# Attention plus mixture of experts on one core: GpSimd's part of the routed slots, unrolled, with its index copies taken out and a weight copy moved in

## What is computed

```python
x = x + gamma * softmax_attention(layernorm(x), ctx, ctx)      # 4 x 512 tokens, 512 wide, 8 heads
t = layernorm(x).reshape(2048, 512)
shared = (silu(t @ sw_gate) * (t @ sw_up)) @ sw_down            # 1408 hidden
top_w, top_i = top_k(softmax(t @ router_w.T), 2)                # 8 experts, 2 for each token
routed[e] = (silu(t @ w_gate[e]) * (t @ w_up[e])) @ w_down[e]   # 352 hidden
out = x + sum_e combine[:, e] * routed[e] + sigmoid(t @ shared_gate_w) * shared
```

## Time and profile before

| | us |
|---|---|
| median of 3 runs | 990.9 (988.89 to 993.4) |
| span of the profiled execution | 980.4 |
| the 39 slots, from the end of the shared expert (about 647) on | about 333 |

### The profile page before, as it was taken

One profiled execution on the slowest core, in us unless ns is written; L12 is line 12 of the kernel. 1 busy time (PEld: TensorE's weight loads), 2 busy tenths in 40 slices (PEclk: granted clock), 3 DMA queues, 4 the chain that ended last, 5 costly groups with the idle time before them and its releaser, 6 DMA issues.

```text
span 980.4 us, 14857 instructions
## 1 busy us (share of the span) xinstructions
PE 887.9 (91%) x4560; PEld 743.1 (76%) x4560; DVE 608.1 (62%) x920; ACT 537.9 (55%) x918; POOL 487.4 (50%) x500
## 2 busy tenths in 40 slices
PE   5798999989989999999999999999888888888993
PEld 3587777778777888888888888888777777777882
DVE  5678787878845633421222121258999998999881
ACT  5588878787855321121121111258777777777781
POOL 5687788777610000273100000027777778887774
PEclk9899999999999999999999999999999999999996
DMA  9334434443633323000400055556333333333333
GB/s 138 80 127 132 134 125 137 120 148 109 226 120 117 97 76 128 1 1 25 118 11 1 0 175 177 177 176 209 66 65 64 64 64 64 64 64 64 65 55 43
DMA packets 70143, 93.78 MB, mean 96 GB/s; under 512 B 16137, under 2 KB 35593, under 8 KB 70098
## 3 DMA queue, kind: packets, MB, share of 16 engines
q1 hardware_dynamic: 60338, 72.73, 24.9%
q0 software_dynamic: 9760, 20.49, 12.1%
HBM read 65.59 MB, written 27.60 MB: 95 GB/s over the span
## 4 chain that ended last, share of the span: by engine, by line
PE 43%; POOL 15%; issue 13%; ACT 2%; POOLq 2%; DMA 2%; DVE 1%; SPq 0%; ACTq 0%; DVEq 0%
PE bank L1348 8%; PE bank L1349 8%; PE bank L1350 8%; POOL sidx L615 5%; POOL wd L631 4%; PE bank L1362 4%; PE bank L1364 4%; PE bank L1363 4%; POOL gidx L607 2%; POOL out L624 2%; POOL xg L610 1%; DMA out<-y,sidx 1%; PE bank L1242 1%; ACT pb L681 1%; PE bank L1415 1%
## 5 line engine op out<-in xcount | busy, mean ns | idle before, releaser
L1036 DVE TENSOR_TENSOR sg<-bank,sg 128x512 f32<-128x512 f32 x44 | 30.4, 692 | 208.7 <-PE bank L1350 200.0
L1348 PE MATMUL bank<-x_hl,wsp 128*128 128x512 f32 x352 | 137.1, 390 | 0.0
L1350 PE MATMUL bank<-x_hl,wsp 128*128 128x512 f32 x352 | 137.0, 389 | 0.0
L1349 PE MATMUL bank<-x_hl,wsp 128*128 128x512 f32 x352 | 136.9, 389 | 0.0
L610 POOL DMA_INDIRECT xg<-x_normed_rows,gidx x39 | 40.9, 1048 | 186.9 <-PE bank L1372 158.8
L1152 DVE TENSOR_TENSOR wg<-wex,wg 128x1408 fp32r<-128x1408 f32 x39 | 112.0, 2871 | 12.4 <-ACT wg L813 12.4
L624 POOL DMA_INDIRECT out<-y,sidx x39 | 96.0, 2462 | 38.4 <-POOL sidx L615 18.4
L787 ACT ACTIVATE sg<-bank 128x512 f32<-128x512 f32 x44 | 26.3, 598 | 158.4 <-PE bank L1350 158.4
L687 ACT ACTIVATE pth<-bank 128x512 fp32r<-128x512 f32 x128 | 73.3, 598 | 49.2 <-PE bank L1242 47.7
L593 POOL DMA_INDIRECT slot_rows<-msrc,posi x32 | 32.8, 1025 | 134.2 <-DVE posi L1143 124.7
L934 DVE TENSOR_TENSOR ptl<-bank,pth 128x512 fp32r<-128x512 f32 x128 | 85.9, 682 | 18.7 <-ACT pth L687 18.4
(11 more groups left out here) (160 smaller groups left out, 2420.0 us busy)
## 6 DMA issues: line engine op xcount, KB each, us to landing
cd<-in_ctx SPq DMA_DIRECT2D x32, 256.0 KB, 4.9
wex<-in_L_ffn_w_gate SPq DMA_DIRECT2D x8, 704.0 KB, 4.4
wex<-in_L_ffn_w_up SPq DMA_DIRECT2D x8, 704.0 KB, 5.8
xb<-in_x SPq DMA_DIRECT2D x16, 256.0 KB, 4.7
cn<-in_ctx SPq DMA_DIRECT2D x16, 256.0 KB, 3.0
x2b<-in_x SPq DMA_DIRECT2D x16, 256.0 KB, 2.7
x_rows<-x2b SPq DMA_DIRECT2D x16, 256.0 KB, 2.1
x_normed_rows<-x2n SPq DMA_DIRECT2D x16, 256.0 KB, 2.0
```

What stands on the lines that cost most here:

```text
L1348: te.matmul(bk[:, :], hi, xhi, start=(h == 0), stop=False)
L1349: te.matmul(bk[:, :], hi, xlo, start=False, stop=False)
L1350: ins = te.matmul(bk[:, :], lo, xhi, start=False, stop=(h == HC - 1))
```

## The change

GpSimd's part of the slots is written out for all 39 slots, with constants in place of registers for slot numbers and waits (the expert's number still comes from a register). The index copies and their tiles and semaphores are gone: both indirect transfers take the index column from `meta`. The tail's hi copy (L849) leaves ScalarE; GpSimd makes it itself, after `e_d3` (TensorE has read the tail of the slot before) in place of after `a_wd`, waits for its own copy (`g_wh`) and then makes the lo part as before.

```diff
-        gidx = [place(f"gidx{j}", [P, 1], I32) for j in range(4)]
-        sidx = [place(f"sidx{j}", [P, 1], I32) for j in range(4)]
...
-            def gather(s, half, j):
-                if not isinstance(s, int) or s >= 4:
-                    wait_ahead(g, ld_xg[j % 2], 16 * (half - 1))
-                gp.tensor_copy(gidx[j % 4][:, :], meta[:, s, 0:1]).then_inc(g_gi, 1)
-                wait_ahead(g, e_tx, s - 1)
-                wait_ahead(g, g_gi, s + 1)
-                g.indirect_dma_start(out=xg[j % 2][:, :], out_offset=None, in_=xn_d,
-                                     in_offset=bass.IndirectOffsetOnAxis(ap=gidx[j % 4][:, 0:1], axis=0)).then_inc(ld_xg[j % 2], 16)
...
-                gp.tensor_copy(sidx[j % 4][:, :], meta[:, s, 0:1]).then_inc(g_si, 1)
...
-            def down_lo(s, e):
-
-                wait_ahead(g, a_wd, s + 1)
+            def gather(s):
+                if s >= 4:
+                    g.wait_ge(ld_xg[s % 2], 16 * (s // 2 - 1))
+                after(g, e_tx, s - 1)
+                g.indirect_dma_start(out=xg[s % 2][:, :], out_offset=None, in_=xn_d,
+                                     in_offset=bass.IndirectOffsetOnAxis(ap=meta[:, s, 0:1], axis=0)).then_inc(ld_xg[s % 2], 16)
...
+                    g.wait_ge(st_y[(s + 1) % 2], 16 * ((s + 1) // 2))
+                g.wait_ge(a_y, s + 1)
+                g.indirect_dma_start(out=out, out_offset=bass.IndirectOffsetOnAxis(ap=meta[:, s, 0:1], axis=0),
+                                     in_=y3[s % 2][:, :], in_offset=None, compute_op=ALU.add).then_inc(st_y[s % 2], 16)
+
+            def down_tail(s, e):
+                after(g, e_d3, s)
+                if s < E:
+                    g.wait_ge(ld_ex[s], 64)
                 c = slice((IC - 1) * H, IC * H)
+                gp.tensor_copy(wd3[0:IR, 0, c], wex[0:IR, e, 2 * W3 + (IC - 1) * H:EW]).then_inc(g_wh, 1)
+                g.wait_ge(g_wh, s + 1)
                 gp.tensor_tensor(wd3[0:IR, 1, c], wex[0:IR, e, 2 * W3 + (IC - 1) * H:EW], wd3[0:IR, 0, c].bitcast(F32), ALU.subtract).then_inc(g_wd, 1)
...
             g.wait_ge(d_r, R_TAB)
-            down_lo(0, 0)
...
-            over_slots(g, slot, reads_experts=True)
+            g.wait_ge(e_d, SC * NB)
+            down_tail(0, 0)
+
+            for i in range(NG):
+                experts = experts_from(g, i)
+                for j in range(min(4, SLOTS - 4 * i)):
+                    s = 4 * i + j
+                    if s + 4 < SLOTS:
+                        gather(s + 4)
+                    if s + 1 < SLOTS:
+                        down_tail(s + 1, experts[j])
+                    scatter(s)
...
-                sc.activation(wd3[:, 0, 0:2 * H], wex[:, e, 2 * W3:2 * W3 + 2 * H], ACT.Copy)
-                sc.activation(wd3[0:IR, 0, 2 * H:D3], wex[0:IR, e, 2 * W3 + 2 * H:EW], ACT.Copy).then_inc(a_wd, 1)
+                sc.activation(wd3[:, 0, 0:2 * H], wex[:, e, 2 * W3:2 * W3 + 2 * H], ACT.Copy).then_inc(a_wd, 1)
```

More of the change, by code:

```diff
@@ L252, in xattn_moe_kernel @@
         ld_meta, ld_xg, st_y = sem("ld_meta"), sems("ld_xg", 2), sems("st_y", 2)
-        g_gi, g_si = sem("g_gi"), sem("g_si")
+        g_wh = sem("g_wh")
         a_wg, d_wg, a_wu, d_wu, a_wd, d_wd, g_wd = sem("a_wg"), sem("d_wg"), sem("a_wu"), sem("d_wu"), sem("a_wd"), sem("d_wd"), sem("g_wd")
@@ L602, in _, with scatter @@
             g.wait_ge(d_wl, SC)
-            def gather(s, half, j):
-                if not isinstance(s, int) or s >= 4:
-                    wait_ahead(g, ld_xg[j % 2], 16 * (half - 1))
-                gp.tensor_copy(gidx[j % 4][:, :], meta[:, s, 0:1]).then_inc(g_gi, 1)
-                wait_ahead(g, e_tx, s - 1)
-                wait_ahead(g, g_gi, s + 1)
-                g.indirect_dma_start(out=xg[j % 2][:, :], out_offset=None, in_=xn_d,
-                                     in_offset=bass.IndirectOffsetOnAxis(ap=gidx[j % 4][:, 0:1], axis=0)).then_inc(ld_xg[j % 2], 16)
-            def scatter(s, half, j):
-                gp.tensor_copy(sidx[j % 4][:, :], meta[:, s, 0:1]).then_inc(g_si, 1)
-                if isinstance(s, int) and s == 0:
+            def gather(s):
[4 more added lines that the diff above has]
+                                     in_offset=bass.IndirectOffsetOnAxis(ap=meta[:, s, 0:1], axis=0)).then_inc(ld_xg[s % 2], 16)
+            def scatter(s):
+                if s == 0:
                     for tt in range(TB):
@@ L620, in scatter @@
                 else:
[L621 to L625, removed]
-            def down_lo(s, e):
-                wait_ahead(g, a_wd, s + 1)
+                    g.wait_ge(st_y[(s + 1) % 2], 16 * ((s + 1) // 2))
[6 more added lines that the diff above has]
+                    g.wait_ge(ld_ex[s], 64)
                 c = slice((IC - 1) * H, IC * H)
+                gp.tensor_copy(wd3[0:IR, 0, c], wex[0:IR, e, 2 * W3 + (IC - 1) * H:EW]).then_inc(g_wh, 1)
+                g.wait_ge(g_wh, s + 1)
                 gp.tensor_tensor(wd3[0:IR, 1, c], wex[0:IR, e, 2 * W3 + (IC - 1) * H:EW], wd3[0:IR, 0, c].bitcast(F32), ALU.subtract).then_inc(g_wd, 1)
             for s in range(4):
-                gather(s, s // 2, s)
+                gather(s)
             g.wait_ge(d_r, R_TAB)
-            down_lo(0, 0)
[L638 to L644, removed]
-            over_slots(g, slot, reads_experts=True)
+            g.wait_ge(e_d, SC * NB)
[9 more added lines that the diff above has]
+                    scatter(s)
         @block.scalar
```

## The result

The changed kernel takes 941.24 us (median of 4 runs, 937.24 to 951.05), the kernel before 992.15 on the same chip (4 runs, 988.89 to 993.69): ratio 0.950, 95% interval 0.9443 to 0.9557, so about 50 us or 5% faster. The forecast was 940.

A forecast was written before the change was run, and what follows sets the result against it. GpSimd and VectorE blocking each other over SBUF were taken to hold slots at 8.24 us. With PE bounding at 6.70, 34 slots save 50.5 and the end 0.5: span 929.4, plus 10.5 gives 940 us, range 934 to 970.

The forecast's parts named there:

- The bound goes over to PE: Slots: PE, with a floor of 6.68 us a slot, becomes the bound; 6.70 taken, 227.8 us for 34 slots.
- The loop as counted: GpSimd and VectorE in each slot, from wg's end: subtraction ends at 5.13, wg 1.50 more, loop 6.63 us.
- What sets the scatter off: Slots: without the sidx copy and its 0.83, the scatter goes off at wg's start, not after wu's; the larger effect.
- gidx's 1.00: Slot loop: gidx copy 0.20 plus dead time 0.80 ahead of the gather go, with 0.31 in their place.
- The old sum of 8.25: Kernel before, one slot from wu's end to the next: scatter, gidx copy, dead time, gather, subtraction, wg, h, wu.
- Who goes first: Rival listed first: order of wd against gather and copy makes slots 7.1 to 7.5 us, 962 to 968 in all; 25%.
- the scatter's row: Earlier trace: a scatter waiting through wu got in at its end although wd stood behind; used against the rival on order.
- Old loop: Rival: scatter still starts after wu has begun, waiting for the previous landing; 8.30 us a slot, 994 in all; 13%.
- slower: Rival: old slot loop with a 0.80 wait for the hi copy; 9.06 us a slot, 1021 in all; 7%.
- The 0.80 belongs to the indirect transfer: Rival: dead time ahead of the gather stays without the index copy; 6.81 us a slot, 944 in all; 10%.
- the stalls for new code: Unrolled GpSimd slots: fetching code might stall 1 to 2 us in some groups, 0 to 15 us; 0 taken.
- The earlier release of wd: Slots: L849 off ScalarE, 0.62 less each, so wd follows wu with no gap; in slot 33 it had waited 0.17.

The follow-up runs named there:

- short_pe_changed: The changed kernel without one product of three in TensorE's gate and up matmuls (output not full): 920.44 us in one run, 6.44 us a slot once steady.
- sidx_moved_ahead: The kernel before, same instructions and loop, with the scatter's index copy ahead of the tail's subtraction instead of behind it: 932.23 us, ratio 0.9517.
- gidx_out_only: The changed kernel with the scatter's index copy and wait put back and the tail's hi copy on ScalarE: 930.64 us, ratio 0.947.
- tail_on_gpsimd_only: The changed kernel with both index copies and their waits put back, tail's hi copy still on GpSimd: 994.54 us, ratio 1.0136 to the kernel before.
- unroll_only: The kernel before with only GpSimd's slot loop written out; index copies stay, ScalarE still makes the tail's hi part: 980.16 us, ratio 0.9996.
- indices_direct: The changed kernel with the tail's hi copy back on ScalarE, leaving unrolling and direct index columns: 927.47 us, ratio 0.9456; run again, 929.55 us.

## Why the prediction was right, point by point

**The bound goes over to PE: right.** 227.8 us were forecast for the 34 slots, 227.36 came. The floor had a row of its own, so it did not depend on the rest of the sum.

**The loop as counted: right in order, 0.18 too long.** Gather end 2.85 and wd end 3.11 were measured at 2.83 and 3.11; 0.31 between the transfers came as read from the earlier trace rows, and the gather ended 0.87 behind wu, where the earlier trace rows had 0.88. This order is the one of nine slots of the changed kernel and of the steady stretch of *short_pe_changed*. The copy behind wd took 0.46 and not 0.57, the wait for it 0.08 and not 0.17. So the subtraction ends at 4.95, not 5.13, and the loop is 4.95 + 1.50 = 6.45, not 6.63; *short_pe_changed* measured 6.44. The room under PE is 0.24 us a slot, not 0.05.

**What sets the scatter off: half right.** The prediction put the gain on the dispatch time of the scatter, and *sidx_moved_ahead* shows this with the same instructions. The prediction went on to treat the sidx copy as the switch and gidx's 1.00 as a plain term, and there it failed: *gidx_out_only* ran at 6.68. The step that failed is "they decide when the scatter is dispatched", said of the sidx copy and its 0.83. A copy costs 0.18 or 1.60, by whether POOL gets its turn before wg, and the 1.00 ahead of it decides that as well. The old sum of 8.25 was the sum of one regime, and its terms couldn't be taken out one at a time.

**Who goes first: it happens, and costs nothing here.** In 28 of 38 slots the copy got in ahead of wd, which was stretched to 1.63, as the first rival had it. But the rival started from a scatter behind wg. Here the scatter is ahead of wg, so all of POOL's work begins about 1.5 us earlier, and the loop fits under PE. The prediction took the scatter's row as a turn won against wd; but wd kept its 1.21 beside it, so there was nothing to win.

**Old loop and slower: not here, but real.** *tail_on_gpsimd_only* shows the long regime with the copy in it: 294 us for the slots, against 282 and 308 in the two rivals. The price of the wait in the slower one (0.80) was wrong: between two computing instructions it is 0.08.

**"The 0.80 belongs to the indirect transfer": wrong.** With the columns direct the gather has 0.31 ahead of it, and the scatter 0.16 behind a subtraction. The rest of the 0.80 belongs to the wait for the copy.

**Tail on POOL, wait on `e_d3`, unrolling: right at nothing.** *unroll_only* has ratio 0.9996, without the stalls for new code that the range allowed for, and *indices_direct* equals the changed kernel. The earlier release of wd (L849 out of ScalarE) can't be seen: in *indices_direct*, with that copy on ScalarE, wd follows wu without a wait of its own too.

**The total: the difference right, the absolute number partly by luck.** Span 980.4 to 939.7 is -40.7: slots -50.9, the end -1.6 (24.78 us from slot 36's last down matmul to the end, 26.41 before, forecast 0.5), and +11.9 from the disturbed stretch of that execution. Without the last the difference is -52.5, forecast -51.0; on another chip the changed kernel has a span of 928.6, forecast 929.4. To the span the sum added 10.5, by which the median lay above it. The changed kernel's profiled execution took 942.02 with a span of 939.7, so only 2.3 lie around a span. If it was so before too, the profiled execution before took about 983 and was quicker than those timed (988.89 to 993.4), and that makes up the other 8 of the 10.5. The changed kernel's profiled execution was not quicker than its median, because of the disturbed stretch; whether the other three had such a stretch no trace shows. So the 940 met executions some 10 us slower than those on the other chips (930.25), and why this chip's were slow, for both kernels, is open. The ratio is the sounder test of the sum: forecast 940.0/990.9 = 0.949; measured 0.950 and, on another chip, 0.9457 (0.9426 to 0.9487).

**A rule of the skill.** The scatter dispatched at 792.86, behind wg (792.75), took 2.98 and ended 1.47 after wg did, where one that is ahead takes 1.60. The Trainium skill, "SBUF — State Buffer", section "Who interferes with whom", infers that a tensor_tensor doesn't stall GpSimd's descriptor work. By this row it holds up the start of a transfer. By the 24 slots above it doesn't hold up the rest: the scatter of 772.41 and the wg of 772.58 ran side by side in their plain times. The prediction took its row against the whole rule, and that is too much. What in the start waits is open.

For computing instructions the order of dispatch decides in the rows shown: the sidx copy takes 1.60 behind wg and 0.18 ahead of it, and wg fell from 3.23 to 1.63 when the subtraction had ended before it. The Trainium skill, "SBUF — State Buffer", section "Summary: rules for kernel authors", has it so: with two SBUF inputs on VectorE's side and a GpSimd instruction that reads SBUF, the second to issue waits for the whole of the first. The earlier trace rows hold an exception: wg was dispatched at 788.20, while the gather ran and 0.45 ahead of the subtraction (788.65), and still the subtraction went first. No run here explains it.

**Left open.** What in a transfer's start waits for VectorE; why the unsteady kernels repeat in patterns of three or four slots, and so how to work out their mean; what stopped PE near 450 us in one execution (it has no releaser in the trace, and wasn't tried); and why the first slots of *short_pe_changed* are uneven. No version here with the full output beats the changed kernel by more than its interval.

## What to carry to other kernels

Where two engines take turns at one resource, read the order of their requests before the durations: ask of each instruction whether it gets its turn before or after the other engine's long one, and of a transfer whether it starts before or after it. Moving a tiny copy past one instruction can be worth what removing it is. Take the floor of the engine that becomes the bound from a stretch in which it already runs without gaps, and measure the new loop by lengthening it or by shortening the cover, since under a full engine loops of different length look the same.

## What the runs showed of the hardware

- GpSimd waiting for its own instruction: 0.08 us idle between two computing instructions (copy to subtraction; 0.17 in the earlier trace rows), 0.80 to 0.84 idle ahead of an indirect transfer that waits for a copy. An indirect transfer with no such wait has 0.16 idle behind a computing instruction and 0.31 behind another transfer.
- An indirect transfer dispatched during a VectorE instruction with two SBUF inputs, 0.05 us or more after its start, ends about 1.48 us (scatter) or 0.87 us (gather) after it. A scatter dispatched ahead of wg isn't slowed and doesn't slow it (24 of 24 slots of the changed kernel from 690 us on); of 24 gathers ahead of wu none is slowed, but three wu beside them took 2.06 and not 1.62.
- When computing instructions of GpSimd and VectorE wait for each other, they take turns: after wu a GpSimd copy goes, then wd, then the subtraction (1.33, 1.63 and 2.15 us where each alone takes about 0.6, 1.2 and 1.3). A copy of 128 numbers that comes after a VectorE request waits for all of it: 1.60 against 0.18.
- Both indirect transfers take their indices as well from a column in the slot table as from a compact tile: gather 0.99, scatter 1.60 where nothing is in their way.
